# Decoder block on one core: the causal mask of self-attention added by VectorE while it copies the turned scores, with new instruction lists on every engine

## The reference

```python
q_c = _rms_norm(x @ wq_down.T, q_norm_w)            # 384 latents per token
q_nope = (q_c @ wq_up.T)...; q_pe = rope(q_c @ wq_rope.T)
kv_c = _rms_norm(x @ wkv_down.T, kv_norm_w)         # 128 latents per token
scores = einsum('bqhd,bkhd->bhqk', q, k) * scale    # 16 heads, 128 + 64 wide
scores = where(causal, scores, -inf); probs = softmax(scores)
x = layernorm(x + (probs @ v) @ wo.T)
# cross-attention: 16 heads of 32, keys and values from ctx (8, 375, 128),
# with the same causal mask over (query, key)
x = layernorm(x + cross_attention(x, ctx))
# feed-forward: 16 experts of width 128, each token to its top 2, and
# 2 shared experts of width 2048, gelu
x = layernorm(x + shared(x) + routed(x))
```

## Time and profile before

| | before |
|---|---|
| runs | 857.64 us median of 3 (856.75 to 858.61) |
| profiled execution | 858.94 us, span 857.1 us |
| mean granted clock of TensorE | 0.996 of full |
| PE busy | 827.0 us, 96% |
| VectorE busy | 518.0 us, 60% |
| ScalarE busy | 470.3 us, 55% |
| POOL busy | 241.7 us, 28% |
| DMA | 99.99 MB, mean 117 GB/s |

### The profile page before, as it was taken

The page is one execution under the profiler, slowest core; times in us unless marked ns, Lnnn a source line. Parts: engine busy times, 40 slices in busy tenths (PEclk is TensorE's granted clock), DMA queues, the critical chain, the costliest instruction groups (busy, mean ns, idle before and its releaser), DMA issues.

```text
span 857.1 us, 13364 instructions
## 1 busy us (share of the span) xinstructions
PE 827.0 (96%) x4302; PEld 706.4 (82%) x4302; DVE 518.0 (60%) x962; ACT 470.3 (55%) x1221; POOL 241.7 (28%) x284
## 2 busy tenths in 40 slices
PE   7999999999999999999998899999999999999997
PEld 5887887888788777888877689888888988889885
DVE  4755654753664548687787566355665655646466
ACT  6427545753843556977785526063755737647050
POOL 0142320230132031655654002602233322321420
PEclk9999999999999999999999999999999999999999
DMA  9113225315132406322120113624563655644422
GB/s 336 67 44 111 74 53 152 121 43 160 73 96 51 153 23 213 87 59 57 50 70 24 53 47 85 259 85 150 174 218 117 229 172 184 199 140 144 130 79 86
DMA packets 41597, 99.99 MB, mean 117 GB/s; under 512 B 15888, under 2 KB 23952, under 8 KB 39920
## 3 DMA queue, kind: packets, MB, share of 16 engines
q1 hardware_dynamic: 30496, 61.62, 23.0%
q0 software_dynamic: 11056, 37.79, 13.6%
HBM read 71.59 MB, written 20.97 MB: 108 GB/s over the span
## 4 chain that ended last, share of the span: by engine, by line
PE 77%; issue 9%; ACT 4%; DVE 4%; SPq 2%; DMA 2%; POOL 1%; POOLq 0%; ACTq 0%; DVEq 0%
PE ps L1545 61%; PE ps L1894 2%; PE ps L1566 2%; PE ps L1778 2%; SPq L556 2%; PE ps L1605 2%; PE ps L1884 1%; ACT Pt L885 1%; PE ps L1709 1%; PE ps L1597 1%; DMA stage<-in_wa 1%; PE ps L1896 1%; PE ps L1632 1%; PE ps L1560 1%; PE ps L1718 1%
## 5 line engine op out<-in xcount | busy, mean ns | idle before, releaser
L642 POOL TENSOR_TENSOR Pt<-Pt,rowinv 112x448 f32<-112x448 f32 x64 | 59.7, 933 | 188.2 <-DVE rowinv L1155 187.8
L1545 PE MATMUL ps<-x2T_hi,ws_hi 128*128 128x448 f32 x256 | 95.8, 374 | 3.7 <-ACT h_hi L1020 3.7
L885 ACT ACTIVATE Pt<-ps,negmax 112x112 f32<-112x112 f32 x256 | 87.1, 359 | 19.3 <-DVE negmax L1148 19.1
L1545 PE MATMUL ps<-x2T_hi,ws_lo 128*128 128x448 f32 x256 | 94.3, 368 | 0.0
L1545 PE MATMUL ps<-x2T_lo,ws_hi 128*128 128x448 f32 x256 | 94.2, 368 | 0.0
L1019 ACT ACTIVATE hf<-ps,b 128x448 f32<-128x448 f32 x64 | 40.5, 633 | 93.0 <-PE ps L1545 73.9
L1545 PE MATMUL ps<-w_hi,h_hi 128*128 128x512 f32 x224 | 89.9, 401 | 0.0
L1545 PE MATMUL ps<-w_hi,h_lo 128*128 128x512 f32 x224 | 88.4, 395 | 0.0
L1545 PE MATMUL ps<-w_lo,h_hi 128*128 128x512 f32 x224 | 88.4, 395 | 0.0
L1092 DVE TENSOR_TENSOR h_lo<-hf,h_hi 128x448 fp32r<-128x448 f32 x64 | 39.8, 623 | 47.0 <-ACT h_hi L1020 46.6
L1431 DVE TENSOR_TENSOR acc<-ps,acc 128x512 f32<-128x512 f32 x56 | 38.6, 689 | 45.0 <-PE ps L1545 38.1
(11 more groups left out here) (291 smaller groups left out, 2225.8 us busy)
## 6 DMA issues: line engine op xcount, KB each, us to landing
stage<-in_wf SPq DMA_DIRECT2D x30, 513.0 KB
rows_in<-in_zeros SPq DMA_DIRECT2D x30, 256.0 KB, 4.1
xs<-rows_in POOLq DMA_DIRECT2D x29, 256.0 KB, 4.3
rows_out<-yb POOLq DMA_DIRECT2D x29, 256.0 KB
stage<-in_wa SPq DMA_DIRECT2D x4, 1408.0 KB, 6.6
stage<-in_wb SPq DMA_DIRECT2D x4, 1280.0 KB, 5.6
qr<-ro_hi SPq DMA_DIRECT2D x64, 56.0 KB, 1.9
qr<-ro_lo SPq DMA_DIRECT2D x64, 56.0 KB, 1.9
```

The source lines that it names most:

```text
L642: nc.gpsimd.tensor_tensor(p, p, rowinv[0:S, b % 2, :].unsqueeze(2).broadcast_to([S, GH, S]), ALU.mult).then_inc(norm_done, 1)
L885: last = nc.scalar.activation(Pt[0:S, b % 2, h * S:(h + 1) * S], ps[0:S, b % 2, h * S:(h + 1) * S], ACT.Exp, bias=negmax[0:S, b % 2, h:h + 1],
L1545: ins = mm(dst, w, x, start=start and i == 0, stop=stop and i == len(ops) - 1, skip_group_check=not (start and stop))
```

## The change

Self-attention's mask leaves PE. G is five matmuls, and its way out of the bank is no copy on ScalarE but an addition on VectorE of the bank and `maskf` (112 x 112 in float32, repeated for four heads). The mask matrix is transposed for this (keys on partitions), so cross-attention, which keeps its mask matmul, has the two operands exchanged. `maskf` now lives through both attentions. In turn 0 job A2 waits for batch 6 or 7 of the latents alone instead of for all eight. In the body of cross-attention POOL's split LK also waits for the V jobs of the group before.

```diff
@@ both = ctx.enter_context(ExitStack())
+        maskf = sb("maskf", [P, S], at=both)
@@ first (the buffers of the beginning)
-        maskf = sb("maskf", [P, S], at=first)
@@ POOL, split_lk
                 if isinstance(g, int):
                     pool.wait_ge(a_free["B"], NG * GH)
+                else:
+                    pool.wait_ge(x_free["V"], XJ.count(("V", 1), g - 1))
@@ ScalarE, att_step
-                elif kind == "G":
-                    act.wait_ge(job_done, at.number + 1)
-                    copy(sT[0:S, j % 2, :], ps[0:S, 6 + at.bank, 0:GH * S]).then_inc(a_free["G"], 1)
@@ VectorE, att_step
+                elif kind == "G":
+                    dve.wait_ge(job_done, at.number + 1)
+                    nc.vector.tensor_tensor(sT[0:S, j % 2, :].rearrange("p (h s) -> p h s", h=GH),
+                                            ps[0:S, 6 + at.bank, 0:GH * S].rearrange("p (h s) -> p h s", h=GH),
+                                            maskf[0:S, :].unsqueeze(1).broadcast_to([S, GH, S]), ALU.add)\
+                        .then_inc(a_free["G"], 1)
@@ PE, att_step
-                    pe.wait_ge(tr_lo, HB if item in PRE_BANK else B)
+                    pe.wait_ge(tr_lo, HB if item in PRE_BANK else 7 + at.bank if kind == "A" else B)
@@ PE, att_step, kind "G"
-                    mask(bank[0:S, 0:GH * S], maskb, identb)
...
-                        ins = mm(heads(bank[0:S, 0:GH * S]), w, x, start=False, stop=i == len(ops) - 1,
-                                 skip_group_check=True)
+                        ins = mm(heads(bank[0:S, 0:GH * S]), w, x, start=i == 0, stop=i == len(ops) - 1)
@@ PE, x_step, kind "S"
-                    mask(ps[0:S, j % 2, 0:GH * S], identb, maskb)
+                    mask(ps[0:S, j % 2, 0:GH * S], maskb, identb)
@@ constants
-    o["mask"] = np.where(np.arange(P)[:, None] < np.arange(S), f(-3.0e38), f(0))
+    o["mask"] = np.where(np.arange(P)[:, None] > np.arange(S), f(-3.0e38), f(0))
@@ the lists, of which these lines stand for all
 X_LAST_ACT = [
-    ("U2", 2), ("U2", 3), ("Z", 7), ("ROOT2", 1), ("FF", 0), ("ROW2", 4), ("ROW2", 5), ("FF", 1), ("FF", 2),
-    ("U2", 4), ("U2", 5), ("U2", 6), ("FF", 3)]
+    ("U2", 1), ("U2", 2), ("U2", 3), ("ROOT2", 1), ("ROW2", 4), ("ROW2", 5), ("FF", 0), ("U2", 4), ("U2", 5),
+    ("U2", 6), ("FF", 1), ("FF", 2), ("FF", 3)]
```

More of the change, by code:

```diff
@@ L91 @@
 NEXT = "+"
[L94 to L106, removed]
 def group_of(item):
@@ L133 @@
 ROWS_ON_ACT = [t for t in range(TT) if t not in ROWS_ON_DVE]
[L136 to L142, removed]
@@ L159 @@
-_pe, _act = [("Z", 2), ("S", 0), ("T", 1), "fill"], [("Z", 2), ("T", 1), ("S", 0), "fill"]
-_dve, _pool = [("S", 0), ("T", 1), ("Z", 2), ("N", 0), "fill"], [("N", 0), "fill"]
-ATT_PE, ATT_ACT, ATT_DVE = (weave(range(10), p, fill=_fill) for p in (_pe, _act, _dve))
-ATT_POOL_PRE = [("KR", 0), ("O", 0), ("R", 0), ("KR", 1), ("O", 1), ("R", 1)]
-ATT_POOL = weave(range(10), _pool, fill={3: [(NEXT, "O", 0)], 4: [(NEXT, "R", 0)], 6: [(NEXT, "O", 1)],
-                                         7: [(NEXT, "R", 1)]})
@@ new lines @@
+ATT_PRE_DVE = [
+    ("LAT", 0), ("LAT", 1), ("LAT", 2), ("LAT", 3), ("RMS", 1), ("KR", 0), ("NAT", 1), ("A", 0), ("A", 1), ("E", 0),
+    ("O", 0), ("LAT", 4), ("LAT", 5), ("LAT", 6), ("LAT", 7), ("KR", 1), ("VAL", 4), ("VAL", 5), ("VAL", 6),
+    ("VAL", 7), ("A", 2), ("E", 1), ("O", 1), ("Q", 0, 0), ("Q", 1, 0), ("Q", 2, 0), ("Q", 3, 0), ("Q", 0, 1),
+    ("G", 0), ("SB", 0), ("Q", 1, 1)]
+ATT_POOL_PRE = [("KR", 0), ("O", 0), ("R", 0), ("KR", 1), ("O", 1), ("R", 1)]
+PRE_BANK = {("A", 0): 2, ("A", 1): 3, ("E", 0): 0, ("O", 0): 1}
@@ new lines @@
+ATT_PE = [
+    ("SB", 1), ("S", 0), ("G", 1), ("Q", 2, 1), ("G", 2), ("S", 1), ("B", 0), ("SB", 2), ("B", 1), ("T", 0), ("S", 2),
+    ("Q", 3, 1), ("B", 2), ("Z", 0), ("T", 1), ("G", 3), ("G", 4), ("Z", 1), (NEXT, "SA", 0), ("S", 3), ("S", 4),
+    ("T", 2), ("G", 5), (NEXT, "O", 0), ("B", 3), ("Z", 2), (NEXT, "SA", 1), ("S", 5), (NEXT, "E", 0), ("T", 3),
+    ("G", 6), ("W", 0), (NEXT, "A", 0), ("G", 7), (NEXT, "SA", 2), ("T", 4), (NEXT, "R", 0), ("Z", 3), ("W", 1),
+    (NEXT, "E", 1), (NEXT, "A", 1), ("S", 6), ("T", 5), ("Z", 4), ("S", 7), ("W", 2), (NEXT, "A", 2), ("Z", 5),
+    (NEXT, "O", 1), (NEXT, "R", 1), ("W", 3), ("T", 6), (NEXT, "Q", 0, 0), (NEXT, "Q", 1, 0), ("T", 7),
+    (NEXT, "Q", 2, 0), ("Z", 6), (NEXT, "SB", 0), ("W", 4), (NEXT, "Q", 3, 0), ("Z", 7), (NEXT, "Q", 0, 1), ("W", 5),
+    (NEXT, "G", 0), (NEXT, "Q", 1, 1), ("W", 6)]
@@ new lines @@
+ATT_DVE = [
+    ("S", 0), ("SB", 1), ("G", 1), ("N", 0), ("Q", 2, 1), ("G", 2), ("SB", 2), ("B", 0), ("S", 1), ("B", 1), ("T", 0),
+    ("N", 1), ("S", 2), ("Q", 3, 1), ("B", 2), ("T", 1), ("Z", 0), ("G", 3), ("N", 2), ("G", 4), ("S", 3),
+    (NEXT, "SA", 0), ("G", 5), ("T", 2), ("N", 3), ("Z", 1), (NEXT, "O", 0), ("S", 4), ("B", 3), (NEXT, "SA", 1),
+    (NEXT, "E", 0), ("G", 6), ("S", 5), (NEXT, "SA", 2), ("T", 3), ("W", 0), ("N", 4), ("Z", 2), (NEXT, "A", 0),
+    ("Z", 3), ("G", 7), ("T", 4), ("N", 5), ("W", 1), (NEXT, "E", 1), (NEXT, "A", 1), (NEXT, "R", 0), ("S", 6),
+    ("T", 5), ("N", 6), ("W", 2), ("Z", 4), (NEXT, "A", 2), (NEXT, "O", 1), ("S", 7), ("W", 3), ("N", 7),
+    (NEXT, "Q", 0, 0), ("Z", 5), ("T", 6), (NEXT, "Q", 1, 0), (NEXT, "Q", 2, 0), ("W", 4), ("T", 7), ("Z", 6),
+    (NEXT, "Q", 3, 0), (NEXT, "R", 1), (NEXT, "Q", 0, 1), (NEXT, "SB", 0), ("W", 5), ("Z", 7), (NEXT, "G", 0),
+    (NEXT, "Q", 1, 1), ("W", 6)]
```

76 lines of the change are left out of this document (37 added, 39 removed), and 60 rows, old and new, of tables (ATT_LAST_ACT, ATT_LAST_DVE, ATT_LAST_PE, ATT_PRE).

## The result

The changed kernel takes 852.27 us (median of 4 runs, 851.61 to 852.93); the kernel before took 857.86 beside it (4 runs). The ratio is 0.9931, 95% interval 0.9919 to 0.9943: 5.6 us faster, where 17.2 were forecast (840.5, range 834 to 850). The time lies outside the range.

What follows compares the result with a forecast made beforehand. TensorE (PE) was taken as the bound, busy 827.0 of 857.1 us. Gains of 6.0 + 4.2 + 2.4 - 1.1 + 5.3 + 0.4 = 17.2 off the 857.64 median gave 840.4, stated as 840.5; range 834 to 850.

Steps and rivals of the forecast that it cites:

- The rest ... nothing on the path: Remaining edits (maskf kept longer, A2's batch wait, cross-attention's mask operands exchanged): no effect on the path.
- the pricing of E0 by VectorE alone: Next head group's first job: waits for O0's two multiplications on VectorE instead of a copy, 0.3 us late.
- Mask off PE, 6.0: Self-attention: 32 mask matmuls leave PE at 0.19 us each, 6.0 us gained; lower bound 2.9.
- The body's waits, 4.2: Self-attention's loop: PE's waits for turned scores shrink, 1.4 us net in each of three turns; bounds 0 and 6.0.
- The last group, 2.4: Self-attention's last head group: 3.5 us of waits go, 1.1 of new ones come, 2.4 gained; bounds 0 and 3.5.
- Cross-attention, -1.1: Cross-attention: the keys' copy comes late behind S5's exponentials on ScalarE, three times, 1.1 us lost; bounds 0 and 4.1.
- The border, 5.3 + 0.4: Border to the feed-forward part: PE's wait before unit 4 and slow clock go, 5.3 us; last batch's wait, 0.4.
- New waits for old (1): Rival: the lists only move PE's waits, so only masks (6.0) and border (5.3) stay; 846.3 us, chance 0.12.
- 2 falls: Rival 2: the border to the feed-forward part does not close; 845.7 us, chance 0.14.
- rival 5: All self-attention waits go and 2.5 us around the last batch; 23.6 gained in all, 834.0 us, chance 0.14.
- Rival 4: Self-attention: PE waits for VectorE's additions behind reciprocals at 32 G jobs; 25.6 us lost, 866 us, chance 0.04.
- Rival 3: Self-attention: POOL's port lock holds VectorE's low parts, 0.6 us a turn, 2.5 in four groups; 842.9 us, chance 0.04.

Runs made afterwards that it cites:

- the queue put right: The changed kernel with only the ten DMAs of zeros moved in SP's queue from the end of a turn to between the two packs: 839.97 us.
- The run with the mask: Mask matmul back on PE ahead of each G, beside VectorE's addition, against the kernel with the zeros between the packs: 842.38 us, 2.4 above it.

## Why the prediction was wrong, step by step

- **The step that failed** is "The rest ... nothing on the path", together with the pricing of E0 by VectorE alone ("now waits for O0's two multiplications"). The lists moved R1 on ScalarE, thus SP's second pack, thus the zeros, past the moment at which `stage` comes free, and the load of wa got behind them. That cost 6.8 in each of two turns, 13.7 in self-attention, and 12.3 between the medians (852.27 less 839.97). Neither a term nor a rival had SP's queue, although the rows for it were in the trace: the load at 148.75 and the zeros until 139.66, 9 us of slack. The sign of being wrong that the prediction named, a turn above 70.5, is what the trace shows (75.5); with the queue put right a turn is 68.5.
- **Mask off PE, 6.0:** 2.4 to 2.5. The price of one mask, 0.19, was right where it stands. Missing was that PE, freed of the masks, comes early to three places a turn at which VectorE is not ready, and to one long wait in the first turn.
- **The body's waits, 4.2:** with the queue put right, the three turns take 207.9 instead of 217.9, 10.0 gained. The run with the mask took 209.8, which leaves 8.1 for the waits, by subtraction: about twice my value and above my bound of 6.0. That bound held only the two listed waits of the third turn. The smaller ones (at 219.78, 222.15 and 226.08, idle for 0.12 or less) went too, with their restarts some 0.9 a turn by the usual distances between starts. The errors of these two terms nearly cancel.
- **The last group, 2.4 (and 1.5 of mask):** 53.25 (286.15 to 339.4) became 48.5, 4.7 against 3.9. Right.
- **Cross-attention, -1.1:** -0.3 to -0.4. By the starts of S0 a turn takes 28.35 instead of 28.24, three times; and behind the last group 4.7 was gained, with 5.1 at the border. The place was right (S0 waits 0.28, 0.21 and 0.17 for the keys); there was more slack than I read.
- **The border, 5.3 + 0.4:** 5.1. Unit 0 waits 1.69 for x2T_lo, and six waits of 0.26 to 0.85 lie around the last tiles, but unit 4 does not wait and the clock stays up. Right; in some executions of the kernels with the same lists the clock does fall once at the border, and that gives about 2 us back.
- **Rivals 1, 2 and 5.** New waits for old (1) is not what the right queue leaves: from the second turn on no wait above 0.15 is listed in the loop. The border closed, so 2 falls. With the queue put right the body gave more than rival 5 allowed it (8.1 against 6.0) and the mask less.
- **Rival 4 (slower by VectorE's queue)** is real as a mechanism: it is what happens with the old lists. The new lists put G1's and G2's additions ahead of the reciprocal and of SB2's low part, and that removes all of it but the three holds of 0.2 a turn.
- **Rival 3 (low parts held by POOL)** names a hold that the traces do show, and more of it than the row's 0.08. In the old lists with the addition on VectorE the low part of SA meets POOL's multiplication in every turn:

```profile
235.96 0.93 POOL L642 TENSOR_TENSOR Pt<-Pt,rowinv 112x448 f32<-112x448 f32 x1 [2.86 <-DVE rowinv L1152]
```
```profile
236.44 1.27 DVE L1089 TENSOR_TENSOR wa_lo<-stage,wa_hi 128x768 fp32r<-128x768 f32 x1
```

It takes 1.27 where it takes 0.96 alone (157.96 above): 0.31 more for an overlap of 0.46. So the lock that the prediction describes is there, though it holds VectorE for less than the overlap of the two records (by about 0.14); the row's 0.08, measured against a mean and for an overlap of only 0.24, spoke against it too strongly. But in the new lists the hold costs nothing to speak of: in the turns of the run with the zeros between the packs only the smallest low part from `stage` meets POOL, once a turn, for 0.05 more (0.73 instead of 0.68). What the hold cost with the old lists was not measured by itself.

With the queue put right the sum of 17.2 stands against 18.0 measured (858.01 less 839.97, on one chip). That it comes so near is partly luck: two errors of opposite sign, 3.6 too much for the mask and 3.9 too little for the waits.

## What to carry to other kernels

When lists move a producer of a DMA, read the whole queue of the engine that issues it, in its order, and compare for each load the moment at which its buffer comes free with the end of whatever stands ahead of it in the queue; work that nobody waits for belongs behind the load that somebody waits for. The producer need not be the job that the change is about: here it was one copy on ScalarE, two engines away from the load. An operation moved to another engine is priced by what stands ahead of it in that queue, not by that engine's share of busy time: the same 32 additions stand in a kernel that is 9.4 us slower than before, in one that is 1.2 slower by seven steps in another order, and in one that is 18 faster, of which 5 are the border's. Work taken off the busiest engine gives back its full price only as long as no other engine has to keep up with it. And a late load costs from the first instruction that stands behind the waiting one, not from the job that needs the data.
